# Expert loops over 71 tiles instead of 72, and one block of semaphore increments less

## The reference

```
x = x + retention(layernorm(x), ...)
x = x + moe(layernorm(x), Wg, bg, w1, w2)
x = x + rwkv6(layernorm(x), ...)
x = x + moe(layernorm(x), Wg, bg, w1, w2)

moe:   logits = t @ Wg.T + bg                 # 8 experts
       topw, topi = top_k(softmax(logits), 2) # shares divided by their sum
       per expert: gate, up = split(t @ w1e.T);  o = (silu(gate) * up) @ w2e.T
       out = sum over a token's two experts of share * o
```

## Time and profile before

| | |
|---|---|
| median of 3 executions | 1417.14 us (1410.76 to 1417.57) |
| the profiled execution | 1415.21 us |
| its span, from the first to the last instruction | 1413.3 us |
| around the span | 1.9 us |
| PE busy | 1159.3 us, 82% of the span |
| DVE busy | 910.4 us, 64% |
| ACT busy | 620.7 us, 44% |
| POOL busy | 551.6 us, 39% |
| `ffn1`, from the barrier behind `ret` to its last barrier | 324.4 to 573.3 us |
| `ffn2`, from the barrier behind `rec` to the end | 1130.9 to 1413.3 us |

### The profile page before, as it was taken

The page is one execution under the profiler, slowest core; times in us unless marked ns, Lnnn a source line. Parts: engine busy times, 40 slices in busy tenths (PEclk is TensorE's granted clock), DMA queues, the critical chain, the costliest instruction groups (busy, mean ns, idle before and its releaser), DMA issues. The chain is left out here.

```text
span 1413.3 us, 34490 instructions
## 1 busy us (share of the span) xinstructions
PE 1159.3 (82%) x13860; PEld 802.2 (57%) x13860; DVE 910.4 (64%) x1889; ACT 620.7 (44%) x1319; POOL 551.6 (39%) x536
## 2 busy tenths in 40 slices
PE   5999999965499999178889899898987647999960
PEld 3566666643388888024555555555554426888850
DVE  4677777656655665448587786968646276556645
ACT  2334343323255555125547364563735233555537
POOL 1233232202177777233241524325051024777750
PEclk9999999988599999589999999999999777999995
DMA  8032222107833333200100000010000095333338
GB/s 309 4 120 92 70 87 85 61 1 265 308 97 102 104 102 98 74 1 31 32 3 32 3 31 25 10 32 3 2 3 2 2 348 189 104 102 102 104 122 309
DMA packets 62441, 126.16 MB, mean 89 GB/s; under 512 B 7632, under 2 KB 43216, under 8 KB 59344
## 3 DMA queue, kind: packets, MB, share of 16 engines
q1 hardware_dynamic: 48464, 86.20, 17.4%
q0 software_dynamic: 13824, 37.77, 8.5%
HBM read 79.90 MB, written 44.04 MB: 88 GB/s over the span
## 5 line engine op out<-in xcount | busy, mean ns | idle before, releaser
L996 POOL DMA_INDIRECT ffn_xs<-xn_rows,ffn_from_row x144 | 139.7, 970 | 131.5 <-DVE ffn_to_row L1371 78.8
L1002 POOL DMA_INDIRECT y_rows<-ffn_ys,ffn_to_row x144 | 142.2, 987 | 51.2 <-issue 36.3
L1153 PE MATMUL ffn_ps_h<-ffn_w_high,ffn_xst 128*128 x576 | 158.2, 397 | 0.5 <-DVE ffn_xst L1404 0.5
L1394 DVE TENSOR_TENSOR ffn_act_in<-ffn_silu_g,ffn_ps_h 128x256 f32<-128x256 f32 x144 | 60.7, 422 | 142.0 <-ACT ffn_silu_g L1036 142.0
L1036 ACT ACTIVATE ffn_silu_g<-ffn_ps_h 128x256 f32<-128x256 f32 x144 | 55.6, 386 | 147.4 <-PE ffn_ps_h L1153 147.4
L1172 PE MATMUL ffn_ps_o<-ffn_w,ffn_act_t 128*128 x288 | 118.9, 435 | 0.5 <-DVE ffn_act_t L1399 0.5
L1153 PEld LDWEIGHTS ffn_ps_h<-ffn_w_high,ffn_xst 128*128 128x128 f32 x576 | 99.2, 191 | 18.6 <-issue 1.3
L1735 POOL TENSOR_TENSOR rec_mixed_w<-rec_mixed_w,rec_xnt 128x512 f32<-128x512 f32 x16 | 17.2, 1090 | 220.7 <-DVE rec_mixed_w L2510 220.7
L1153 PE MATMUL ffn_ps_h<-ffn_w_low,ffn_xst 128*128 x288 | 91.5, 399 | 0.0
L548 DVE TENSOR_TENSOR ret_probs<-ret_score,ret_causal 128x2048 f32<-128x2048 f32 x32 | 73.3, 2292 | 21.5 <-PE ret_score L412 21.5
L261 POOL TENSOR_TENSOR ret_roped<-ret_rope_t 128x512 f32<-128x512 f32 x32 | 40.6, 1267 | 105.1 <-DVE ret_rope_t L541 105.1
(11 more groups left out here) (319 smaller groups left out, 2811.8 us busy)
## 6 DMA issues: line engine op xcount, KB each, us to landing
home<-y_rows SPq DMA_DIRECT2D x20, 512.0 KB, 5.4
ffn_w_high<-w_split SPq DMA_DIRECT2D x8, 1024.0 KB, 9.0
ffn_w_low<-w_split SPq DMA_DIRECT2D x8, 1024.0 KB, 10.9
ffn_w<-w_split SPq DMA_DIRECT2D x8, 1024.0 KB, 14.2
ret_w_raw<-in_f_w SPq DMA_DIRECT2D x12, 512.0 KB, 5.9
w_split<-ret_w_high SPq DMA_DIRECT2D x12, 512.0 KB, 2.6
w_split<-ret_w_low SPq DMA_DIRECT2D x12, 512.0 KB, 4.6
xn_rows<-home SPq DMA_DIRECT2D x10, 512.0 KB, 11.7
```

The source lines that it names most:

```text
L996: pool.indirect_dma_start(xs[:, n % UNROLL, :], None, xn_rows[:], bass.IndirectOffsetOnAxis(ap=from_row[:, n:n + 1], axis=0)) \
L1002: pool.indirect_dma_start(y_rows[:], bass.IndirectOffsetOnAxis(ap=to_row[:, m:m + 1], axis=0), ys[:, m % UNROLL, :], None).then_inc(ys_sto ...
L1153: mm = pe.matmul(ps_h[:, u % 2, :], one_pass(xst[:, u % 2, part, k, :]), one_pass(w1[w_part][k][:, bass.ds(e, E_COLUMNS)]), start=(part + ...
L1394: dve.tensor_tensor(act_in[:, u % 2, :], silu_g[:, u % 2, :], ps_h[:, u % 2, FF:2 * FF], ALU.mult) \
```

## The change

`NTILES` becomes 71, the exact bound, and a new `PADDED` keeps the 72 for the packed expert numbers. All loops over tiles and all tables with a column per tile have 71. The block with the four increments is gone; the four semaphores start at zero, and every wait on them is one lower. In the loop, `output` now waits for its `act_t` itself, where before only the last two did so. Other waits, which were written as 32 or as a multiple of `TURNS` are written as counts of what is loaded or stored, with the same meaning.

```diff
-NTILES = -(-(TOPK * TILES + NE - 1) // UNROLL) * UNROLL
+NTILES = TOPK * TILES + NE - 1
+PADDED = -(-NTILES // UNROLL) * UNROLL
...
-        expert_f = sb("expert_f", [P, LAG + NTILES + 1])
-        experts_f = sb("experts_f", [P, NTILES // UNROLL])
-        experts_of = sb("experts_of", [P, NTILES // UNROLL], mybir.dt.int32)
+        expert_f = sb("expert_f", [P, LAG + PADDED + 1])
+        experts_f = sb("experts_f", [P, PADDED // UNROLL])
+        experts_of = sb("experts_of", [P, PADDED // UNROLL], mybir.dt.int32)
...
-        starts_at_one = [xst_ready, act_ready, act_t_ready, ys_ready]
...
-        with nc.Block() as block:
-            @block.sync
-            def _(sp):
-                for s in starts_at_one:
-                    sp.sem_inc(s, 1)
...
-                    sp.wait_ge(ys_stored[u], 16 * TURNS)
+                    sp.wait_ge(ys_stored[u], 16 * len(range(u, NTILES, UNROLL)))
...
-                        pool.wait_ge(ys_ready, 1 + m + 1)
+                        pool.wait_ge(ys_ready, m + 1)
...
                 def transpose_act(n, u):
-                    pe.wait_ge(act_ready, 1 + n + 1)
-                    pe.wait_ge(act_t_ready, 1 + n)
+                    pe.wait_ge(act_ready, n + 1)
+                    if n >= 1:
+                        pe.wait_ge(act_t_ready, n)
...
                 def output(n, u, e):
-
+                    pe.wait_ge(act_t_ready, n + 1)
                     if n >= 2:
-                        pe.wait_ge(ys_ready, 1 + n - 1)
+                        pe.wait_ge(ys_ready, n - 1)
...
-                    for u in range(UNROLL):
-                        n = turn * UNROLL + u
-                        if not first or u >= 1:
-                            transpose_act(n - 1, (u - 1) % UNROLL)
-                        if not last or u + 2 < UNROLL:
-                            transpose_x(n + 2, (u + 2) % UNROLL)
...
+                    for n in range(turn * UNROLL, min((turn + 1) * UNROLL, NTILES)):
+                        if n >= 1:
+                            transpose_act(n - 1, (n - 1) % UNROLL)
+                        if n + 2 < NTILES:
+                            transpose_x(n + 2, (n + 2) % UNROLL)
...
-                        for u in range(UNROLL - LAG, UNROLL):
-                            pe.wait_ge(act_t_ready, 1 + turn * UNROLL + u + 1)
-                            output(turn * UNROLL + u, u, offset[turn * UNROLL + u])
+                        for n in range(NTILES - LAG, NTILES):
+                            output(n, n % UNROLL, offset[n])
...
-                    digits = expert_f[:, k:k + NTILES - UNROLL + 1:UNROLL]
+                    digits = expert_f[:, k:k + PADDED - UNROLL + 1:UNROLL]
```

More of the change, by code:

```diff
@@ L890, in experts @@
         ROUNDS = STEPS // 4
-        TURNS = NTILES // UNROLL
+        TURNS = PADDED // UNROLL
         GROUPS = 4
@@ L1187, in turn_of_loop @@
                 def turn_of_loop(turn):
-                    first, last = turn == 0, turn == TURNS - 1
                     packed = experts_at(turn)
-                    for u in range(UNROLL):
-                        n = turn * UNROLL + u
-                        if not first or u >= 1:
-                            transpose_act(n - 1, (u - 1) % UNROLL)
-                        if not last or u + 2 < UNROLL:
-                            transpose_x(n + 2, (u + 2) % UNROLL)
-                        if first and u == LAG:
-                            pe.wait_ge(w2_loaded, 16 * len(second_loads))
-                        if not first or u >= LAG:
-                            output(n - LAG, (u - LAG) % UNROLL, offset[n - LAG])
-                        if not last or u + 1 < UNROLL:
-                            offset[n + 1] = expert(packed, LAG + u + 1)
-                            hidden(n + 1, (u + 1) % UNROLL, offset[n + 1])
-                    if last:
-                        transpose_act(NTILES - 1, UNROLL - 1)
-                        for u in range(UNROLL - LAG, UNROLL):
-                            pe.wait_ge(act_t_ready, 1 + turn * UNROLL + u + 1)
-                            output(turn * UNROLL + u, u, offset[turn * UNROLL + u])
+                    for n in range(turn * UNROLL, min((turn + 1) * UNROLL, NTILES)):
+                        if n >= 1:
+                            transpose_act(n - 1, (n - 1) % UNROLL)
+                        if n + 2 < NTILES:
+                            transpose_x(n + 2, (n + 2) % UNROLL)
+                        if n == LAG:
+                            pe.wait_ge(w2_loaded, 16 * len(second_loads))
+                        if n >= LAG:
+                            output(n - LAG, (n - LAG) % UNROLL, offset[n - LAG])
+                        if n + 1 < NTILES:
+                            offset[n + 1] = expert(packed, LAG + n % UNROLL + 1)
+                            hidden(n + 1, (n + 1) % UNROLL, offset[n + 1])
+                    if turn == TURNS - 1:
+                        transpose_act(NTILES - 1, (NTILES - 1) % UNROLL)
+                        for n in range(NTILES - LAG, NTILES):
+                            output(n, n % UNROLL, offset[n])
                 pe.wait_ge(route_step, EXPERTS_OF)
@@ L1412, in turn_of_loop @@
                 def turn_of_loop(turn):
-                    first, last = turn == 0, turn == TURNS - 1
-                    for u in range(UNROLL):
-                        n = turn * UNROLL + u
-                        gate(n, u)
-                        if not first or u >= 1:
-                            act_low(n - 1, (u - 1) % UNROLL)
-                        if not last or u + 2 < UNROLL:
-                            x_low(n + 2, (u + 2) % UNROLL)
-                        if not first or u >= LAG:
-                            y_out(n - LAG, (u - LAG) % UNROLL)
+                    for n in range(turn * UNROLL, min((turn + 1) * UNROLL, NTILES)):
+                        gate(n, n % UNROLL)
+                        if n >= 1:
+                            act_low(n - 1, (n - 1) % UNROLL)
+                        if n + 2 < NTILES:
+                            x_low(n + 2, (n + 2) % UNROLL)
+                        if n >= LAG:
+                            y_out(n - LAG, (n - LAG) % UNROLL)
                 for n in range(2):
```

29 lines of the change are left out of this document (14 added, 15 removed).

## The result

The median went from 1412.42 us (1408.85 to 1417.57, 5 runs) to 1403.80 us (1402.96 to 1405.45, 5 runs): ratio 0.9933, 95% interval 0.9907 to 0.996, which is 0.67% faster. Two later comparisons of the same changed kernel, with 12 runs each, gave 0.9949 (0.9926 to 0.9972) and 0.9945 (0.9918 to 0.9973). The profiled execution took 1404.32 us, its span is 1402.5 (1413.3 before).

The account below looks back on a forecast made before the run. PE's streaming was taken to bound the expert loops at 2.507 us a tile. Tiles 5.0, block 1.5 and tables 0.2 sum to 6.7 us, giving 1409.5 us (mean of 1408.5 and 1410.4), range 1403.5 to 1414.5.

Parts of the forecast that it names:

- the coin's toss: Verdict near a coin's toss, since 6.7 us is just short of 0.5%, 7.1 us; faster 0.41, same 0.56, slower 0.03.
- One tile less, twice: Expert loops of `ffn1` and `ffn2`: one full PE-paced step of 2.507 us goes from each, saving 5.0 us.
- The tables of 72 columns lose one column; that is nothing: Small routing tables on DVE in the expert stages: one column fewer was costed at nothing.
- The block: Block of increments between clears and next block: removal saves 1.0 us in `ffn1` and 0.5 in `ffn2`, 1.5 in all.
- DVE's late start in `ffn1`: DVE starts 0.45 us behind the second release in `ffn1`, 0.1 in `ffn2`; delay kept in the forecast, saving 1.0, not 1.4.
- the rival in which the delay stays: After the barrier branch, the delay passes to what comes next: `ffn1` saves 0.5, sum 6.2 us, result 1410.0; chance 0.05.
- The tables: Routing tables on DVE, 1152 to 1136 elements: 0.09 us a stage, 0.2 in all; odd 71 columns might cost 0.2.
- The second wait: At `output`, costed at 0; rival on PE's path: 6.9 us at 51 ns (0.03) or 20.5 at 0.15 us (0.03).
- The clock at the loops' start: PE's clock rise may shift, 1.3 us more or less a stage, result 1407 to 1412; chance 0.17 larger gain, 0.10 smaller.
- The tail takes the tile back: At the loops' end POOL's scatter backlog decides, so only blocks and tables save: 1.7 us, 1414.5; chance 0.02.

Follow-up runs that it names:

- The runs with a filler: Changed kernel with an unused tile ahead of the loop's buffers: 64 bytes, ratios 0.9948 and 0.9932; 32, 0.9948; 128, 0.9959; 192, 0.9951 and 0.9946.
- the second group: Runs on one unstalled chip moving the loop's buffers in the changed kernel or the kernel before, plus the changed kernel again; kernel before 1416.51 us, ratios 0.9948 to 0.9997.
- at 192 bytes: Changed kernel with an unused 192-byte tile ahead of the loop's buffers; ratios 0.9951 and, run again, 0.9946 (median 1471.39 us).
- the changed kernel's last run: Changed kernel, unchanged, run in the fourth group on a chip where loops stall; ratio 0.9945 to the kernel before, median 1471.19 us.

## Why the prediction came out as it did

The forecast was 1409.5 us, with 1403.8 measured, within the range; the likeliest verdict was "within 0.5%", and it was 0.67%. The forecast's ratio, 1410.4 / 1417.14 = 0.9953, lies within all three intervals measured for this kernel. So the size of the forecast was not refuted, and the verdict was the coin's toss that the text named. Of the 5.7 us between forecast and result 3.7 go with the kernel before itself, whose median was 1417.14 from three runs and 1412.42 from five: the forecast's ratio on the latter gives 1405.8. But the sum came out near by luck: its largest term was half of what it said, and a stage that the prediction put at nothing, `rec`, gave more than was missing.

- **One tile less, twice: 5.0 us. This is the step that failed.** The tile is gone and its successor in the loops' end costs what it did, but the remaining tiles grew by 20 ns each, 2 x 70 x 0.020 = 2.8 us, so that 2 x 1.17 = 2.3 us came from the loops apart from their start. "The tables of 72 columns lose one column; that is nothing" was true of their own instructions and false of what is allocated behind them. The runs with a filler, and the kernel before moved by 192 bytes, show it from both sides: the loops apart from their start give 4.6 us with the buffers moved back, and are 2.7 us longer in the kernel before with the buffers moved away.
- **The block: 1.5 us.** 2.16 - 1.14 + 1.62 - 1.13 = 1.51, and with the block put back these came back. I kept DVE's late start in `ffn1`; it went as well (0.45 to 0.12 us), but `ffn1`'s norm started only 0.17 earlier for it. That 0.17 us is the block's too: from the last release to the norm it is 3.20 to 3.21 us in the kernels with the block and 3.02 to 3.03 in those without, in every profile. So the block was worth 1.7 us, and the rival in which the delay stays is refuted: the delay didn't pass on to what comes next. The Trainium skill (Runtime: NRT & Kernel Launch, "Instruction fetch mechanics") has a taken branch wait for a DMA if its target isn't among the instructions that the engine holds. Whether DVE's delay was such a wait, no run shows.
- **The tables: 0.2 us.** The big ones went from 0.75 to 0.74 us as worked out, and `second_at`, now 71 columns wide, takes 0.20 us as before, so the odd width cost nothing:

```profile
367.44 0.74 DVE L1335 TENSOR_TENSOR ffn_in_its_tile<-ffn_number_table,ffn_tile_of 128x1136 bf16<-128x1136 bf16 x1
...
372.09 0.20 DVE L1356 TENSOR_SCALAR ffn_second_at<-ffn_choice 128x71 f32<-128x71 f32 x1
```

  The way to the first gather gave 0.89 us nevertheless. Besides the 0.17 of the block, PE's last routing products, which `choice_at` waits for, ran at a higher granted clock, here in `ffn2` before (1.89 us, granted clock 0.59) and after (1.24 us, 1.00):

```profile
1176.35 1.89 PE L1134 MATMUL ffn_ps_o<-ffn_number,home 128*128 128x144 bf16 x16 [0.39 <-DVE ffn_number L1350]
```

```profile
1166.33 1.24 PE L1127 MATMUL ffn_ps_o<-ffn_number,home 128*128 128x142 bf16 x16 [0.87 <-DVE ffn_number L1340]
```

- **The second wait: nothing.** Right, though I doubted it on the way. It is there 138 times (the prediction counted 136), its 51 ns a microsecond ahead of the weights it guards, and the kernels that have it with the buffers at the old place run at 2.508 us:

```profile
L1162 PEldq EVENT_SEMAPHORE  x1: 51/51/51, 1291.4 to 1291.4; - x1
```

```profile
L1166 PEld LDWEIGHTS ffn_ps_o<-ffn_w,ffn_act_t x2: 189/190/190, 1292.7 to 1293.0; 128*128 128x128 f32 x2
```

- **The clock at the loops' start**, a rival at 1.3 us a stage: it moved as described, -1.2 in `ffn1` and +0.2 in `ffn2`. I had looked for the clock's chance there alone. The larger one is in `rec`, 12 us between the extremes, with no line of the change near it: the sum has no term for it, the profile shows -6.6 us there, and that is what made the measured change larger than the sum while the tiles gave less.
- **The tail takes the tile back:** no. From the last `hidden` to the end the stages took 0.2 us more in sum.

What stays open: the expert stages account for 4.5 us, the medians for 7 to 9, each with an interval of 3 to 4 us to either side. In the second group, a straight line through each kernel's times against the mean granted clock of the run falls by 0.8 to 1.0 us for 0.001 of clock; read at 0.924 it gives 1413.4 us for the kernel before (33 runs) and 1408.3 for the changed one (12 runs), 5.1 apart. That speaks for some 5 us of the change and the rest of chance. The same line gives 1407.0 us for the changed kernel moved by 64 bytes and 1415.2 for the kernel before moved by 192: 1.3 us below and 1.8 above the same kernels unmoved, the way their steps go, but no more than the scatter. If the loops' pace itself shifts the mean clock, as the section before leaves open, reading all at one clock takes a part of the effect away or adds one. No run separates it further. Whether the version moved by 64 bytes is faster than the changed kernel isn't settled by times either (1408.08 against 1407.50, 1470.75 against 1471.19); by the expert stages of the profile it is 3 us ahead of the changed kernel.

## What to carry to other kernels

A change in the size of one table moves all that is allocated behind it. Where PE streams without a wait, compare its step to the nanosecond before and after, and if it has changed with no instruction changed, put an unused tile ahead of the buffers and look again. Cut a profile at its barriers before a difference of the span is credited to the change: here a stage that it doesn't touch gave more than the ones that it does. And a median step over a loop with stalls is no price of an instruction.

## What was not expected of the hardware

- The byte position of the loop's buffers in SBUF changes PE's pace: 2.507 to 2.552 us for the same 14 matrix products, 1.8%. By the distances of the weight loads it lies in the products that read `xst` and `act_t`: the second and the third load of `hidden` are 0.225 us apart before, 0.229 after and 0.234 at 192 bytes, while the two loads of `transpose_x` stay 0.108 to 0.109 apart. Why wasn't found. That `ffn2` has 2.514 and `ffn1` 2.508 us at the same place, in one profile, says that place isn't all: there `hidden` takes 1.273 us instead of 1.255 and `output` 0.681 instead of 0.692. ACT and DVE write these buffers while PE reads them; whether PE meets them there, or its own reading depends on the address, no run separates.
- The same program took 1416.5 us on the chip of the second group and 1477.7 to 1479.6 on the two chips of the others. The difference is in the expert loops. There, in the changed kernel's last run, DVE's product waits for nothing the profile names or for ACT, which had itself been held up:

```profile
DVE ffn_act_in L1384 <- ACT ffn_silu_g L1031: 30.1, 21, 3.7
DVE ffn_act_in L1384 <- issue: 19.2, 10, 3.6
```

  No more than eight steps in a row are undisturbed. Apart from the loop's start, the long ones (2.7 to 6.6 us, some twenty in each loop) begin with the ninth or tenth step and then come mostly every three or four tiles, in all of these kernels. A pattern that belongs to the program and a cost that belongs to the place where it runs would fit the fetching of the unrolled loop's code, but the packets on the queue of instructions give no sign of it: 116 without stalls (the changed kernel's first profile) and 116 with them (its last), and their time no larger a share of the longer span. No run tested it.

```profile
q8 instruction: 116, 1.90, 0.6%
```

```profile
q8 instruction: 116, 1.90, 0.5%
```
